# A Mamba and mixture-of-experts block: two-best ranking in three VectorE passes, and ScalarE's decays issued seven units ahead of the scans

## The reference

```python
h = layernorm(x) * (1 + ca) + sa
x = x + ga * mamba(h)          # conv, silu, x_proj, softplus, selective scan, gate, out_proj
h = layernorm(x) * (1 + cb) + sb
x = x + gb * ffn(h)            # shared expert + 8 routed experts, the two best weighted
```

```python
h = h * exp(d_t * A) + (d_t * u_t) * b_t      # exp(d_t * A) is the "decay"
y_t = sum_n h[n] * c_t[n]
```

```python
probs = softmax(flat @ router_w + router_b)
topk_probs, topk_idx = lax.top_k(probs, 2)
weights = zeros.at[rows, topk_idx].add(topk_probs)
```

## Time and profile before

| | us |
|---|---|
| median of three executions | 687.82 |
| lowest, highest | 684.22, 689.11 |
| the profiled execution | 684.8 |
| its span, first to last instruction | 683.1 |

### The profile page before, as it was taken

How to read it: one execution, slowest core, us unless ns; L and a number is a source line. 1 busy time by engine, 2 the same in 40 slices (tenths; PEclk the granted TensorE clock), 3 DMA queues, 4 the chain that set the end, 5 groups by cost and what they waited for, 6 DMA issues and landing times.

```text
span 683.1 us, 9767 instructions
## 1 busy us (share of the span) xinstructions
PE 593.3 (87%) x3646; PEld 466.5 (68%) x3646; DVE 598.3 (88%) x713; ACT 489.7 (72%) x861; POOL 320.2 (47%) x171
## 2 busy tenths in 40 slices
PE   5684478899989998999989998999979947998897
PEld 4243345689657965788567966787668936798686
DVE  5399999999999999999999999999998999798416
ACT  3689535999589976989589957998598925962460
POOL 1036556446654556446653656446543664464000
PEclk9787589999999999999999999999999968999999
DMA  7423333314432235133531343223522442220000
GB/s 221 161 92 140 123 139 142 125 70 169 163 128 82 108 128 184 62 124 124 173 124 63 124 160 138 83 103 124 179 103 70 176 156 83 103 78 16 1 1 16
DMA packets 26705, 77.87 MB, mean 114 GB/s; under 512 B 3025, under 2 KB 17570, under 8 KB 18466
## 3 DMA queue, kind: packets, MB, share of 16 engines
q1 hardware_dynamic: 26178, 76.82, 31.1%
q10 hardware_dynamic: 480, 0.43, 0.2%
HBM read 74.61 MB, written 2.62 MB: 113 GB/s over the span
## 4 chain that ended last, share of the span: by engine, by line
PE 53%; DVE 31%; issue 7%; ACT 5%; POOL 2%; DMA 1%; DVEq 0%; POOLq 0%; ACTq 0%
DVE state L1206 15%; PE psum L677 12%; PE psum L516 10%; DVE psum L1197 8%; PE psum L543 5%; PE psum L645 5%; PE psum L647 4%; PE psum L646 4%; PE psum L687 3%; POOL state L433 2%; PE psum L662 2%; PE psum L565 1%; ACT L866 1%; DVE out_sb L1244 1%; PE psum L799 1%
## 5 line engine op out<-in xcount | busy, mean ns | idle before, releaser
L433 POOL TENSOR_TENSOR state<-state,bc 128x1024 f32<-128x1024 f32 x127 | 300.1, 2363 | 291.8 <-DVE psum L1197 291.8
L1206 DVE TENSOR_TENSOR_SCAN state<-decay,psum 128x1024 f32<-128x1024 f32 x128 | 292.2, 2283 | 21.9 <-PE psum L516 9.5
L885 ACT ACTIVATE decay<-delta,a_neg 128x511 f32<-128x511 f32 x256 | 166.1, 729 | 10.4 <-DVE state L1206 10.3
L516 PE MATMUL psum<-ident,state 128*128 128x128 f32 x1024 | 139.0, 283 | 33.6 <-POOL state L433 33.4
L1197 DVE TENSOR_TENSOR psum<-bc,du 128x1024 f32<-128x1024 f32 x128 | 157.6, 1231 | 4.8 <-DVE state L1206 0.5
L516 PEld LDWEIGHTS psum<-ident,state 128*128 128x128 f32 x1024 | 120.3, 146 | 56.0 <-POOL state L433 44.9
L677 PE MATMUL psum<-down_w,h 128*128 128x128 f32 x896 | 109.9, 276 | 0.0
L677 PEld LDWEIGHTS psum<-down_w,h 128*128 128x128 f32 x896 | 104.4, 192 | 5.3 <-issue 5.3
L1014 ACT ACTIVATE h<-psum,vec 128x512 f32<-128x512 f32 x144 | 97.0, 688 | 2.1 <-PE psum L647 0.6
L980 ACT ACTIVATE gT_mix<-psum,w 128x128 f32<-128x128 f32 x224 | 64.8, 388 | 20.0 <-PE psum L687 14.4
L645 PE MATMUL psum<-h_hi,up_hi 128*128 128x512 f32 x144 | 59.2, 411 | 10.7 <-DVE h_lo L1310 6.7
(11 more groups left out here) (151 smaller groups left out, 638.3 us busy)
## 6 DMA issues: line engine op xcount, KB each, us to landing
bc<-bc_rows SPq DMA_DIRECT2D x64, 1024.0 KB, 4.7
x_sb<-_attn_hidden_states_dram SPq DMA_DIRECT2D x9, 256.0 KB, 2.8
x<-_attn_hidden_states_dram SPq DMA_DIRECT2D x7, 256.0 KB, 3.0
out_dram<-out_sb SPq DMA_DIRECT2D x7, 256.0 KB, 2.4
h<-in_L_ffn_rw_dram SPq DMA_DIRECT2D x1, 1024.0 KB
bc_rows<-rows SPq DMA_DIRECT2D x8, 64.0 KB, 4.8
h<-in_L_wmod_dram ACTq DMA_DIRECT2D x1, 384.0 KB
h<-in_L_attn_in_proj_w_dram SPq DMA_DIRECT2D x1, 256.0 KB, 4.7
```

Source lines behind the costliest of these rows:

```text
L433: pool.tensor_tensor(state[:, u % STATE_RING, :, :], state[:, u % STATE_RING, :, :], bc[:, pair % BC_RING, 1, first:first + NU, :], ALU.mu ...
L516: last = nc.tensor.matmul(Y[q][:, t * P:(t + 1) * P], state[:, u % STATE_RING, s, t * P:(t + 1) * P], ident[:, :], start=False, stop=(u in ...
L885: last = nc.scalar.activation(decay[:, r, s, 1:L], delta[:, b.p, q, 1:L], ACT.Exp, scale=a_neg[:, q, k:k + 1])
L1206: nc.vector.tensor_tensor_scan(state[:, u % STATE_RING, :, :].rearrange("p n t -> p (n t)"), decay[:, u % DECAY_RING, :, :].rearrange("p n ...
```

## The change

`top2` multiplies each probability by a constant tile `tie_scale` (f32, 1 - 2^-24 where the other expert comes earlier, 1 elsewhere), compares "other is greater" against that product, and sums. Five passes over 128x256 elements become three, each waiting for the one before.

`AHEAD` goes from 6 to 7. In ScalarE's queue the slot now has `decays(b, 7)` ahead of `h2_rows` and `decays(b, 8)` behind it (two in place of four), the loop has `decays(b, 9 + j)` for j = 0 to 6 (seven in place of six, the new one, unit 15, at j = 6 ahead of `h_rows(m)` and `mix_scaled(a, 6)`), and the end has `decays(n, 3)` to `(n, 6)` (four in place of three). In sum ScalarE issues the same instructions. The order on the other engines stays.

```diff
-AHEAD = 6
+AHEAD = 7
...
-        before = sb("before", [P, E, E], mybir.dt.bfloat16)
+        tie_scale = sb("tie_scale", [P, E, E])
...
-            pool.memset(before[:, :, :], 1.0).then_inc(const_made, 1)
+            pool.memset(tie_scale[:, :, :], 1.0 - 2.0 ** -24).then_inc(const_made, 1)
...
                 if b:
                     decays(b, AHEAD)
+                if a:
+                    h2_rows(a)
+                if b:
                     decays(b, AHEAD + 1)
-                if a:
-                    h2_rows(a)
-                if b:
-                    decays(b, AHEAD + 2)
-                    decays(b, AHEAD + 3)
...
                 for j in range(DOWNS - 1):
-                    if b and j < DOWNS - 2:
-                        decays(b, AHEAD + 4 + j)
+                    if b:
+                        decays(b, AHEAD + 2 + j)
...
-                mine = pr[:, :, :].unsqueeze(3).broadcast_to([P, NT, E, E])
-                other = pr[:, :, :].unsqueeze(2).broadcast_to([P, NT, E, E])
-                nc.vector.tensor_tensor(gt_eq[:, 1, :, :, :], other, mine, ALU.is_equal
-                                        ).then_inc(prob_step, 1)
-                nc.vector.tensor_tensor(gt_eq[:, 0, :, :, :], other, mine, ALU.is_gt
-                                        ).then_inc(prob_step, 1)
+                nc.vector.tensor_tensor(
+                    gt_eq[:, 1, :, :, :], pr[:, :, :].unsqueeze(3).broadcast_to([P, NT, E, E]),
+                    tie_scale[:, :, :].unsqueeze(1).broadcast_to([P, NT, E, E]),
+                    ALU.mult).then_inc(prob_step, 1)
+                dve.wait_ge(prob_step, k + 4)
+                nc.vector.tensor_tensor(
+                    gt_eq[:, 0, :, :, :], pr[:, :, :].unsqueeze(2).broadcast_to([P, NT, E, E]),
+                    gt_eq[:, 1, :, :, :], ALU.is_gt).then_inc(prob_step, 1)
                 dve.wait_ge(prob_step, k + 5)
-                nc.vector.tensor_tensor(
-                    gt_eq[:, 1, :, :, :], gt_eq[:, 1, :, :, :],
-                    before[:, :, :].unsqueeze(1).broadcast_to([P, NT, E, E]),
-                    ALU.mult).then_inc(prob_step, 1)
-                dve.wait_ge(prob_step, k + 6)
-                nc.vector.tensor_tensor(gt_eq[:, 0, :, :, :], gt_eq[:, 0, :, :, :],
-                                        gt_eq[:, 1, :, :, :], ALU.add).then_inc(prob_step, 1)
-                dve.wait_ge(prob_step, k + 7)
                 nc.vector.tensor_reduce(rank[:, :, :], gt_eq[:, 0, :, :, :], AX.X,
                                         ALU.add).then_inc(prob_step, 1)
```

More of the change, by code:

```diff
@@ L412, in _ @@
                                channel_multiplier=1).then_inc(const_made, 1)
-            pool.affine_select(out=before[:, :, :], in_=before[:, :, :], pattern=[[1, E], [-1, E]],
-                               compare_op=ALU.is_gt, fill=0.0, base=0,
+            pool.affine_select(out=tie_scale[:, :, :], in_=tie_scale[:, :, :],
+                               pattern=[[1, E], [-1, E]],
+                               compare_op=ALU.is_gt, fill=1.0, base=0,
                                channel_multiplier=0).then_inc(const_made, 1)
@@ L1040, in slots @@
                     decays(b, AHEAD)
-                    decays(b, AHEAD + 1)
                 if a:
@@ L1044, in slots @@
                 if b:
-                    decays(b, AHEAD + 2)
-                    decays(b, AHEAD + 3)
+                    decays(b, AHEAD + 1)
                 if a:
@@ L1264, in top2 @@
             def top2(a):
-                k = 8 * a.i
+                k = 6 * a.i
                 dve.wait_ge(router_exp, a.i + 1)
@@ L1275, in top2 @@
                 dve.wait_ge(prob_step, k + 3)
-                mine = pr[:, :, :].unsqueeze(3).broadcast_to([P, NT, E, E])
-                other = pr[:, :, :].unsqueeze(2).broadcast_to([P, NT, E, E])
-                nc.vector.tensor_tensor(gt_eq[:, 1, :, :, :], other, mine, ALU.is_equal
-                                        ).then_inc(prob_step, 1)
-                nc.vector.tensor_tensor(gt_eq[:, 0, :, :, :], other, mine, ALU.is_gt
-                                        ).then_inc(prob_step, 1)
-                dve.wait_ge(prob_step, k + 5)
-                nc.vector.tensor_tensor(
-                    gt_eq[:, 1, :, :, :], gt_eq[:, 1, :, :, :],
-                    before[:, :, :].unsqueeze(1).broadcast_to([P, NT, E, E]),
-                    ALU.mult).then_inc(prob_step, 1)
-                dve.wait_ge(prob_step, k + 6)
-                nc.vector.tensor_tensor(gt_eq[:, 0, :, :, :], gt_eq[:, 0, :, :, :],
-                                        gt_eq[:, 1, :, :, :], ALU.add).then_inc(prob_step, 1)
-                dve.wait_ge(prob_step, k + 7)
+                nc.vector.tensor_tensor(
[6 more added lines that the diff above has]
+                    gt_eq[:, 1, :, :, :], ALU.is_gt).then_inc(prob_step, 1)
+                dve.wait_ge(prob_step, k + 5)
                 nc.vector.tensor_reduce(rank[:, :, :], gt_eq[:, 0, :, :, :], AX.X,
                                         ALU.add).then_inc(prob_step, 1)
-                dve.wait_ge(prob_step, k + 8)
+                dve.wait_ge(prob_step, k + 6)
                 nc.vector.scalar_tensor_tensor(out=w9[:, :, 0:E], in0=rank[:, :, :], scalar=1.5,
```

## The result

| | before | changed |
|---|---|---|
| median of ten executions, us | 684.85 | 691.69 |
| lowest, highest, us | 683.83, 693.44 | 688.85, 693.43 |
| span of the profiled execution, us | 683.1 | 689.9 |

The ratio of the changed kernel to the one before is 1.0071, 95% interval 1.0039 to 1.0103: slower by 0.7%, which is clear of no change. By that ratio the loss is 4.9 us. The medians are further apart, 6.8 us, and the means 4.6 us (691.48 and 686.86): three of the ten executions of the kernel before took 689 to 693 us, the other seven 683.8 to 687.8. VectorE does less and the kernel takes longer. The profiled span has grown by 6.8 us, over twice the 2.5 us of the prediction's sum.

What follows compares the result with a forecast made beforehand. It took a 75.0 us circle through VectorE, ScalarE and TensorE, with scan 7 waiting for TensorE, as the bound. Terms 0, 0 and +2.5 us gave 687.3 us profiled, 690.3 us median; own range 689 to 692, 8-in-10 range 685.0 to 693.5.

Steps and rivals of the forecast that it cites:

- Three passes are worth 0: top2 on VectorE: 0.80 us less in each of seven slots, all lost in scan 7's wait for y_add.
- VectorE's saving shows: Rival: VectorE's shorter top2 shortens the run by 5.6 us, or 3.1 with the pair's cost; chance 0.10.
- Two decays fewer ahead of the gelus are worth 0: ScalarE ahead of h2_rows and router_e: both wait anyway; gain between 0 and 0.1 us a slot, taken as 0.
- One pair at j = 6 costs 0.54 us: ScalarE ahead of mix_scaled(a, 6): 1.22 us of decays less 0.68 slack delays gate_y by 0.54 us, in five slots.
- The pair at the end costs 0, with 1.4 us of cover: decays(n, 6) behind acc_rows on ScalarE: delays the first x_silu, hidden while the second waits for conv_in(n, 1).
- Into the last slots and the tail it does not reach: The j = 6 delay costs 0 in the last slot: no conv_in there, and y_add waits 2.54 us for GpSimd.
- The sum: Whole kernel: 684.8 + 0 + 0 + 2.5 = 687.3 us profiled, 690.3 us on the median's scale, +0.4%.
- The rival in which the pair is hidden: Rival: ScalarE idle time or slack at gate_y absorbs the j = 6 pair; 687.8 us, chance 0.15.
- The rival in which the end of the slot binds: Rival: the fourth pair at the end makes x_silu late, 1.76 us in five slots; 696.6 us, chance 0.07.

Runs made afterwards that it cites:

- the loosened order: Kernel before with three passes, y_add(b, 3) ahead of the up matmuls, acc_transpose behind the next conv_in(n, 0), make_delta behind scan 8: 675.48 us, ratio 0.9833.
- the spare work: Changed kernel plus five spare Exp activations of 128x511 ahead of decays(n, 3) to (n, 6) at the end of each slot: 696.54 us, ratio 1.0142.

## Why the prediction was right, and where it was short

The direction, the place and the size a slot came out as predicted. That the median of 691.69 us lies inside the forecast's own range of 689 to 692 us is in part luck: the base, 687.82 us from three executions, was 3.0 us above the 684.85 us of ten, and the sum of 2.5 us fell short of the loss (4.9 us by the ratio, 6.8 by the medians). The two errors have opposite signs. Point by point:

- *Three passes are worth 0.* Right, by the wait of scan 7, which went from 0.52 to 1.27 us (predicted 1.32), and by the kernel with this piece alone. In the last slot of that kernel the wait grew by less, from 4.01 to 4.45 us. The pass with the f32 tile takes 0.42 us, as the others.
- *VectorE's saving shows* was the rival, and wrong for this order, at 88% busy. In the loosened order, at the same 88%, the saving shows with 0.80 us a slot. The occupancy does not tell the two cases apart; the chain and the scan's wait do. The Trainium skill, Perfetto Trace Analysis, section Identifying the Most-Contended Engine, says to optimise the engine with the highest occupancy first; the runs agree with that for the loosened order and not for the kernel before.
- *Two decays fewer ahead of the gelus are worth 0.* Right: `router_e` waits 1.31 us for the logits, with its release unchanged.
- *One pair at j = 6 costs 0.54 us.* Right. From `mix_scaled(a, 5)` to `acc_rows` it is 322.87 - 315.76 = 7.11 us. Before, `acc_rows` started at 396.18, and `mix_scaled(a, 5)` in ScalarE's timeline of the kernel before, just ahead of those rows, at

```profile
389.61 1.19 ACT L980 ACTIVATE gT_mix<-psum,w 128x128 f32<-128x128 f32 x4
```

  which makes 6.57 us, and the difference 0.54. The period shows the same when each piece is compared with its own partner: 75.52 - 74.98 = 0.54 us with three passes, 75.56 - 75.03 = 0.53 with five. Five slots, 2.5 us: right.
- *The pair at the end costs 0, with 1.4 us of cover.* Right in the sum; the cover is 1.51 us up to the second `x_silu` and another 0.95 us up to `x_proj` (it starts at 333.69, the second `x_silu` ends at 332.74), which I had left out: 2.5 us, as the spare work showed.
- *Into the last slots and the tail it does not reach.* Right for the pair. The tail's 2.7 us stand where the clock fell, and the three passes alone had such a tail too.
- *The sum.* Here the step failed: it had no term for TensorE's clock. The prediction costed every stretch at the durations of one execution, in which the `up` matmuls ran at the upper level in all slots but the last. In the changed kernel's profile two slots and the tail lost 0.8, 0.7 and 2.7 us where the level was the lower one, 4.3 us, more than the pair's 2.5. The rows that would have asked for the term were there: three executions of before from 684.22 to 689.11 us, 4.9 us apart, which I took for scatter without a cause. Freed of the base, the forecast's own range is 1.2 to 4.2 us of loss (689 to 692 from 687.82). The measured 4.9 us (0.71% of 684.85, interval 2.7 to 7.1) lie beyond it, and inside the full range (up to 5.7 us). The profiles and the ratios point to more falls with this change than without it; why, stays open.

The rival in which the pair is hidden was wrong for this order, and becomes half true in the loosened one. The rival in which the end of the slot binds was wrong, with 2.5 us of cover left.

## What to carry to other kernels

Before an engine's work is cut, look at what ends its next wait behind the cut: if that wait is there in every slot, the saving lands in it, however busy the engine is, and the gain comes only when the wait is removed too. When work is moved within a queue that nothing overtakes, price each place by the idle time between it and the next instruction that another engine waits for: the same 1.22 us pair cost 0.54 us ahead of `mix_scaled(a, 7)` and nothing behind `acc_rows`, as long as the cover there lasts. And price a stretch of TensorE at both levels of its clock where the executions of a kernel scatter by more than the change is worth.

## What the runs showed of the hardware

The granted clock fell to the lower level for a few us in some slots and not in others with the same instructions and nearly the same times, and 0.8 us of a slot went with it where it met the `up` matmuls, which take 0.63 us each in place of 0.40. The same fall 9 us behind `gate_y` cost nothing, until 14 more transposes stood there: then it cost 0.5 to 0.7 us (steps of 76.02, 74.43 and 74.42 us). More transposes ahead of them brought the tail back to 53.4 us and the executions to within 3.7 us of each other (685.55 to 689.24). Two decay activations of 128x511 cost 1.22 to 1.23 us from start to start in each row above where the next instruction followed without a wait. The start of the first `gate_y` lay between 108.5 and 112.0 us over the profiled executions of these eleven kernels whose work up to there hardly differs, which is more than the 2.5 us of the pair; the steps from slot to slot separate such effects.
